# VectorE copies the denominators between two halves of statistics, and makes the turned context's remainders ahead of the query's second remainder

## The reference

```
x = x + _L0_xattn_ref(_layernorm(x), ctx_4096, ...)   # attention over 1024 positions, channels of 128
x = x + _L0_ffn_ref(_layernorm(x), ...)               # routed scales, product with the sign of a 1024x1024 weight
x = x + _L1_xattn_ref(_layernorm(x), ctx_4096, ...)   # attention over the 128 rows of the context
x = x + _L1_ffn_ref(_layernorm(x), ...)               # routed low-rank product

def _L0_xattn_ref(x, init, Wq, bq, Wk, bk, Wv, bv):
    q = jnp.einsum('dc,bct->btd', Wq, init) + bq
    k = jnp.einsum('dc,bct->bdt', Wk, init) + bk[None, :, None]
    attention = jax.nn.softmax(jnp.einsum('btd,bds->bts', q, k), axis=-1)
    v = jnp.einsum('oc,bct->bto', Wv, x) + bv
    return jnp.einsum('bts,bsc->bct', attention, v)
```

## Time and profile before

| | us |
|---|---|
| runs: median (lowest to highest) of 3 | 2137.94 (2137.7 to 2138.79) |
| profiled execution: time, and its span | 2137.82, 2136.0 |
| PE busy | 2096.3 (98% of the span) |
| PEld busy | 1726.6 (81%) |
| DVE busy | 1815.6 (85%) |
| ACT busy | 1173.9 (55%) |
| POOL busy | 263.9 (12%) |
| granted TensorE clock | 0.997 of full speed |

### The profile page before, as it was taken

One profiled execution on the slowest core, in us unless ns is written; L12 is line 12 of the kernel. 1 busy time (PEld: TensorE's weight loads), 2 busy tenths in 40 slices (PEclk: granted clock), 3 DMA queues, 4 the chain that ended last, 5 costly groups with the idle time before them and its releaser, 6 DMA issues.

```text
span 2136.0 us, 37755 instructions
## 1 busy us (share of the span) xinstructions
PE 2096.3 (98%) x12759; PEld 1726.6 (81%) x12759; DVE 1815.6 (85%) x3033; ACT 1173.9 (55%) x1786; POOL 263.9 (12%) x306
## 2 busy tenths in 40 slices
PE   9989999999999999999999999999999999999998
PEld 7867888878888888888888888888887888888786
DVE  8258898888889888888899888889888888898885
ACT  4145555655555566555556655555566555556542
POOL 0001111111111111110111011111111111111100
PEclk9999999999999999999999999999999999999999
DMA  6764343344534334453433445343343435333320
GB/s 212 219 197 158 109 141 118 109 160 144 167 108 156 123 105 147 137 167 128 156 115 107 132 137 167 128 157 130 112 126 133 157 128 171 124 122 122 112 70 31
DMA packets 161155, 290.53 MB, mean 136 GB/s; under 512 B 14208, under 2 KB 62608, under 8 KB 161104
## 3 DMA queue, kind: packets, MB, share of 16 engines
q1 hardware_dynamic: 161104, 289.87, 41.9%
HBM read 223.75 MB, written 25.17 MB: 117 GB/s over the span
## 4 chain that ended last, share of the span: by engine, by line
PE 69%; DVE 17%; issue 5%; ACT 2%; DVEq 0%; POOL 0%; ACTq 0%; POOLq 0%
PE acc L1320 8%; PE acc L1281 6%; PE scores L1260 6%; DVE p_lo L1106 6%; PE shared L1294 6%; PE acc L1282 6%; PE acc L1283 6%; PE shared L1295 6%; PE shared L1240 4%; PE scores L1309 4%; PE scores L1308 4%; DVE p_sum L1114 3%; PE shared L1516 3%; PE scores L1246 3%; DVE res L1146 2%
## 5 line engine op out<-in xcount | busy, mean ns | idle before, releaser
L1106 DVE TENSOR_TENSOR p_lo<-prob,p_hi 128x1024 fp32r<-128x1024 f32 x256 | 312.3, 1220 | 128.0 <-ACT p_hi L877 86.0
L870 ACT ACTIVATE prob<-scores 128x1024 f32<-128x1024 f32 x256 | 260.5, 1017 | 227.6 <-PE scores L1309 176.2
L973 DVE TENSOR_REDUCE neg_max<-scores 128x1 f32<-128x1024 f32 x256 | 307.0, 1220 | 43.0 <-PE scores L1260 41.4
L756 POOL TENSOR_TENSOR rstd<-var_eps,minus_half 128x1 f32<-128x1 f32 x128 | 126.8, 991 | 1720.5 <-DVE var_eps L963 1720.5
L1281 PE MATMUL acc<-cT_hi,m_ring 128*128 128x256 f32 x1024 | 302.8, 296 | 0.9 <-DVE x L1007 0.9
L1282 PE MATMUL acc<-cT_lo,m_ring 128*128 128x256 f32 x1024 | 288.5, 282 | 0.0
L1283 PE MATMUL acc<-cT_hi,m_ring 128*128 128x256 f32 x1024 | 288.2, 281 | 0.0
L877 ACT ACTIVATE p_hi<-prob 128x1024 fp32r<-128x1024 f32 x256 | 271.4, 1060 | 29.7 <-PE acc L1320 23.4
L1294 PE MATMUL shared<-signT,y_hi 128*128 128x512 f32 x512 | 205.5, 401 | 0.9 <-DVE y_lo L1013 0.9
L1308 PE MATMUL scores<-q_hl,k_hh 128*128 128x512 f32 x512 | 201.2, 393 | 1.9 <-DVE q_m L1088 1.5
L1281 PEld LDWEIGHTS acc<-cT_hi,m_ring 128*128 128x128 f32 x1024 | 195.5, 191 | 8.4 <-DVE x L1007 1.1
(11 more groups left out here) (243 smaller groups left out, 4098.4 us busy)
## 6 DMA issues: line engine op xcount, KB each, us to landing
m_ring<-m_units SPq DMA_DIRECT2D x512, 256.0 KB, 3.2
xn<-in_x SPq DMA_DIRECT2D x32, 512.0 KB, 4.2
x<-in_x SPq DMA_DIRECT2D x32, 512.0 KB, 5.0
c_val<-in_ctx SPq DMA_DIRECT2D x32, 512.0 KB, 3.9
out_x<-oscale SPq DMA_DIRECT2D x32, 512.0 KB, 3.0
c_in<-in_ctx SPq DMA_DIRECT2D x31, 512.0 KB, 3.3
c_odd<-in_ctx SPq DMA_DIRECT2D x16, 512.0 KB, 4.1
q_m<-q_hl SPq DMA_DIRECT2D x32, 256.0 KB, 3.1
```

The lines of the kernel that those rows point to most:

```text
L973: nc.vector.tensor_reduce(neg_max[:, t:t + 1], scores[t % 2][:, :], AX_X, ALU.max, negate=True).then_inc(row_max, 1)
L1106: nc.vector.tensor_tensor(p_lo[s % 2][:, :], prob[s % 2][:, :], p_hi[s % 2][:, :].bitcast(F32), ALU.subtract).then_inc(p_lo_ready, 1)
```

## The change

On VectorE alone, three things change in iterations that both prepare and attend (k = 1 to 31):

- The denominators' copy is made between the first half of the statistics and the rest, instead of behind all of them.
- The context's two remainders come ahead of the query's second remainder instead of behind it.
- The inverse denominators stand where they stood, behind query remainder 0, and so directly ahead of the context's remainders.

No instruction is added or taken away, and no semaphore's meaning changes. In iteration 1 there are no statistics of the chain, in iteration 31 no context remainders, and in 0, 32 and 33 the order is the old one.

```
--- before.py
+++ after.py
@@ -983,6 +983,12 @@
                                                    k_hh[DQK:P, half(h)].bitcast(F32), ALU.add,
                                                    ALU.subtract).then_inc(k_ready, 1)
 
+                def query_remainder(b, h):
+                    dve.wait_ge(q_hi_ready, nth(2, b, h + 1))
+                    nc.vector.scalar_tensor_tensor(q_hl[DQK:P, half(h)], scores[0][0:DQK, half(h)], bqk_col[0:DQK, :],
+                                                   q_hl[0:DQK, half(h)].bitcast(F32), ALU.add,
+                                                   ALU.subtract).then_inc(q_ready, 1)
+
                 def second_half(i, c, to, src):
 
                     dve.wait_ge(shift_ready[i], nth(1, c, 1))
@@ -1149,19 +1155,19 @@
                         denominators_wide(a)
                     if chain:
                         dve.wait_ge(x3_ready, nth(2, c, 2))
-                        statistics(dve_chain, 3, c, res)
+                        statistics_first(3, c, res)
+                    if attend and prepare:
+                        denominators_wide(a)
+                    if chain:
+                        statistics_rest(dve_chain, 3, res)
                     if chain and not attend:
                         second_half(3, c, xn_3, res)
-                    if attend and prepare:
-                        denominators_wide(a)
                     if prepare:
-                        for h in range(2):
-                            if attend and h == 1:
-                                denominators_inverse(a)
-                            dve.wait_ge(q_hi_ready, nth(2, b, h + 1))
-                            nc.vector.scalar_tensor_tensor(q_hl[DQK:P, half(h)], scores[0][0:DQK, half(h)], bqk_col[0:DQK, :],
-                                                           q_hl[0:DQK, half(h)].bitcast(F32), ALU.add,
-                                                           ALU.subtract).then_inc(q_ready, 1)
+                        query_remainder(b, 0)
+                    if prepare and attend:
+                        denominators_inverse(a)
+                    if prepare and not attend:
+                        query_remainder(b, 1)
                     if attend and not prepare:
                         denominators_inverse(a)
                     if prepare and not attend:
```

## The result

| | median us | lowest to highest | runs |
|---|---|---|---|
| before | 2138.03 | 2137.48 to 2141.05 | 10 |
| after | 2144.51 | 2143.25 to 2145.24 | 10 |

After takes 1.0026 times as long as before, 95% interval 1.0018 to 1.0034: 6.5 us slower, where 2146.6 was forecast. The profiled execution of after took 2144.87 us.

The account below looks back on a forecast made before the run. PE, busy 98%, was the engine to save, but DVE was as full in this stretch and paced it; 0.30 us delay x 29 turns = 8.7 us, iterations 1 and 31 zero, gave 2146.6 us, range 2137 to 2150.5.

Parts of the forecast that it names:

- L1006: DVE instruction behind the second query remainder: starts at 1038.17 to 1038.27 instead of 1037.82, 0.35 to 0.45 us late.
- DVE's stop: At the moved copy, DVE stands idle 0.53 us for the last denominators matmul, delaying everything queued behind.
- PE's gain: PE's waits at L1326 (0.31) and second half of xn_3 (0.18): at most 0.49 us a turn to be had.
- The wait has moved from the copy to the inverse: PE's load for L1491: waits for the inverse denominators until 1036.21, 0.1 us later than before.
- 0.27 to 0.37 is left, and I take 0.30: DVE's delay per turn reaching L1021's end, after slack at L1189 takes up 0.08 to 0.20 us.
- The sum: Whole run: 29 turns x 0.30 = 8.7 us, so 2146.6 us, 0.4% slower.
- Iterations 1 and 31: I take zero.: First and last changed iterations add nothing: 1 has no statistics, in 31 L1491 waits for the inverse again.
- costs nothing itself: DVE's swap of remainder and context: no cost, as the same three instructions stand between the same two.
- Its signs: DVE idle 0.5 us before copy; PE's wait moved to den_inv; L1021 wait 0.3 or more; copies 62.0 us apart.
- PE keeps its gain: Rival at L1491: with DVE's stop under 0.12, PE keeps 0.31 a turn, 9.0 us, 2129 us; chance 0.10.
- the whole stop counts: Rival: DVE's 0.53 reaches L1021 in full because ACT's L802 is late; 15.4 us, 2153 us; chance 0.06.
- The Trainium skill's advice: Cited for the faster rival (2129 us, chance 0.10): bring forward what ends PE's gaps, without asking what the mover gives up.

Follow-up runs that it names:

- stop_only: Against before: nothing moved, but DVE made to wait for the denominators between the two halves of the statistics; 2155.28 us.
- copy_first: Against after: the denominators' copy put ahead of both halves of the statistics; 2162.60 us.
- inv_first: Against after: the inverse denominators put ahead of query remainder 0; 2144.99 us.
- fill: Against after: query remainder 0 put between the first half of the statistics and the denominators' copy; 2155.18 us.
- swap_only: Against after: the copy put back behind all the statistics, the new order of the remainders kept; 2132.57 us.
- copy_only: Against after: the context's remainders put back behind the query's second remainder, the copy's new place kept; 2154.81 us.
- mid: Against after: the copy one instruction later, behind the second half's statistics and before they are combined; 2130.53 us.

## Why the prediction was right, point by point

The mechanism held: DVE stands still for the denominators, PE's wait moves to the inverse, and the delay reaches L1021. Its size did not hold as well: the iterations bring 5.2 us where 8.7 were forecast, and the total of 6.5 lies nearer to the forecast because of time outside them that was put at zero, which is luck. Times of after are brought to before by 3.61.

| step | forecast | measured |
|---|---|---|
| copy on DVE | 1033.63 | 1037.24 - 3.61 = 1033.63 |
| variance L963 | 1035.00 | 1035.00 |
| L789 | 1036.15 | 1036.15 |
| load for L1491, now L1499 | 1036.21 | 1036.22 |
| L802 | 1037.58 | 1037.57 |
| second half of `xn_3` | 1037.72 | 1041.40 - 3.61 = 1037.79 |
| L1006, now L1012 | 1038.17 to 1038.27 | 1038.28 |
| end of L1021, now L1027 | 1048.69 | 1050.86 + 1.40 - 3.61 = 1048.65 |
| PE's load behind it | 1048.74 | 1048.70 |

- **DVE's stop.** 0.53 was forecast; the trace marks 0.45 of it as idle, and the rest is L955's end, which no successor overlaps (1036.09 + 0.61 would have been L959's start; 1037.24 - 1036.70 = 0.54). That it costs was forecast and is shown by stop_only and copy_first.
- **PE's gain.** "The wait has moved from the copy to the inverse" is in the trace as forecast. inv_first adds what the prediction did not say: without that wait the gain is lost as well, at the second half of `xn_3`, which ACT sets: it starts 0.12 behind the end of L789 in both.
- **L1006.** It starts at the upper end of its bounds since ACT's L802 sets it, not DVE's own queue, which would have been ready at 1040.97 + 0.74 = 1041.71, or 1038.10. The prediction used ACT's time only for a bound. fill shows that this path has no more room.
- **The mis-sized term: "0.27 to 0.37 is left, and I take 0.30".** The period grew by 0.18. In iteration 15's turn 0.26 is left. In the next turn PE's L1472 stands at 1098.49 against 1094.65, and DVE's logits,

```profile
1107.84 0.15 DVE L1197 TENSOR_TENSOR logit<-shared,br_rows 128x8 f32<-128x8 f32 x1
```

  at 1107.84 - 3.84 = 1104.00 against 1103.81, so only 0.19 is left of the 0.46 or so with which L1006 starts late there too. The two kinds of turn alternate (in after the denominators come 61.93 and 61.83 us apart, in before 61.70 each time), and the forecast took the slack of iteration 15, 0.08, for all 29, although it names the 0.20 of the next turn beside it. Besides, L1189 before had waited for PE and started only 0.79 behind L955; in after its semaphore is up and it starts 0.61 behind (1046.00 - 1045.39), so its slack was 0.18 in iteration 15 and 0.29 in 16, larger than the idle time that the rows marked.
- **The sum.** 29 x 0.18 = 5.2 and not 8.7, hence 2143 where 2146.6 stood; measured were 2144.5. The profiled executions lie 2143.1 - 2136.0 = 7.1 us apart, and 1.3 of these lie in the start: the first copy comes at 173.59 in after, at 172.26 in before. Over all profiled kernels it comes between 172.3 and 175.7, without a pattern that follows the edits, and inv_first has it at 172.79 with the same median as after. What sets it stays open.
- **"Iterations 1 and 31: I take zero."** For 31 this is wrong, by 0.5 to 0.6 us. PE's denominators and L1006 (L1012) in iteration 31, before:

```profile
2020.23 0.61 PE L1464 MATMUL scores<-prob,ones 128*32 128x256 f32 x8
...
2025.03 0.69 DVE L1006 TENSOR_TENSOR prob<-acc,prob 128x512 f32<-128x512 f32 x1 [1.31 <-ACT prob L802]
```

  and after:

```profile
2026.73 0.61 PE L1472 MATMUL scores<-prob,ones 128*32 128x256 f32 x8
...
2032.21 0.69 DVE L1012 TENSOR_TENSOR prob<-acc,prob 128x512 f32<-128x512 f32 x1 [1.48 <-ACT prob L802]
```

  The denominators are 6.50 apart, and the spans 7.1, so some 0.6 comes behind them. ACT has no context to round there and already waits for POOL's shift in before (0.75 us at L789), so the later variance goes through to L802 and L1006: 5.48 behind the denominators instead of 4.80. The prediction looked at PE's loads alone in this iteration.
- **The swap "costs nothing itself".** Right, and too little said: it is the only part of the change that gains (swap_only). The prediction priced PE's 0.18 at the second half of `xn_3` at most as a part of the 0.49, and did not say that alone it would come through: 29 x 0.18 = 5.2, against 5.6 measured. Nor did it say that the early copy without the swap would cost 16.7 (copy_only).
- **Its signs.** Of those it named, DVE's idle time, the moved wait and the missing wait for a context remainder came. The copies are 61.89 apart and not 62.0, and PE's wait for L1021 in the turn is 0.24 and not 0.3 or more. This last sign tells nothing: in mid, which is faster than before, PE's wait for the results is 10.0 us in all and 43 times, as in after.
- **The rivals.** That PE keeps its gain needed a stop of DVE under 0.12: after didn't have it, mid has it, at 2130.53 against the 2129 of that rival. The one by which the whole stop counts (2153) is wrong for after, and nearly describes copy_only and stop_only, where no swap makes room.
- **The Trainium skill's advice** weighed there ("Perfetto Trace Analysis", section "Optimization Strategy": find the gaps of the most-contended engine and let what ends them come sooner) came true in mid (2130.53) and failed in after (2144.51). What ended the gap came sooner in both; in after the engine that brings it had to stand still for that, 0.45 us a turn.

## What to carry to other kernels

An instruction that another engine waits for is moved up in its queue only to the place at which its own semaphore is just up. Here, with the remainders swapped in all three, the copy in its old place gave 5.6 us (swap_only), behind the second half of the statistics 7.6 (mid), and one place further up it lost 6.5 (after). Everything behind a waiting instruction is late by the wait, so count first who waits for those, and on which paths (here DVE's own queue, the one over POOL and ACT, and the one over PE's loads that wait for the remainders). The largest new wait in a list may be harmless (inv_first took 14 us of it away for nothing); put each part of a change on the chip alone, since a gain and a loss can lie on top of each other.

## What was not expected of the hardware

In these rows an instruction of DVE that needn't wait starts before the one ahead has ended, and one whose semaphore comes late loses that too. L1197 starts 0.61 us behind L955 (0.69 long) when its semaphore is already up. In the earlier trace rows L1189 starts 0.79 behind it, and the 0.10 between the two is not marked as idle time. So a wait costs DVE here some 0.1 us more than the gap between the two instructions (0.54 and not 0.45 at the copy), and a short gap goes unmarked. In mid the copy starts 0.59 behind L959 and the combination 0.34 behind the copy, which took 0.41.
